# A masked sum moved into a later batch, a maximum over partitions by TensorE, and two activations in the other order

## What is computed

```python
x = x + tanh(g_xattn[0]) * attention0(layernorm(x), ctx)
x = x + tanh(g_ffn[0]) * ffn0(layernorm(x))      # base + update * 0.5
x = x + tanh(g_xattn[1]) * attention1(layernorm(x), ctx)
x = x + tanh(g_ffn[1]) * ffn1(layernorm(x))
# ffn0: the update goes through the sum over e of coefs[e] * mask[e] (e = 0, 1, 2)
# ffn1: x_scale = 448 / max(abs(x2)); w_scale = 448 / max(abs(weight))
#       out = fp8(x2 * x_scale) @ fp8(weight * w_scale) / (x_scale * w_scale)
```

## Time and profile before

| | us |
|---|---|
| median of 3 runs (lowest, highest) | 1494.67 (1492.06, 1496.3) |
| time of the profiled execution | 1496.8 |
| its span in the profile | 1495.1 |
| PE busy in the span | 1377.2 (92%) |
| DVE busy | 971.4 (65%) |
| ACT busy | 745.9 (50%) |
| POOL busy | 426.3 (29%) |

### The profile page before, as it was taken

One profiled execution on the slowest core, in us unless ns is written; L12 is line 12 of the kernel. 1 busy time (PEld: TensorE's weight loads), 2 busy tenths in 40 slices (PEclk: granted clock), 3 DMA queues, 4 the chain that ended last, 5 costly groups with the idle time before them and its releaser, 6 DMA issues. The chain is left out here.

```text
span 1495.1 us, 28528 instructions
## 1 busy us (share of the span) xinstructions
PE 1377.2 (92%) x10782; PEld 1120.8 (75%) x10782; DVE 971.4 (65%) x1564; ACT 745.9 (50%) x1881; POOL 426.3 (29%) x473
## 2 busy tenths in 40 slices
PE   6998789989989999987999999999779999999388
PEld 6998778979889898865888888888556666666144
DVE  4363277777767767565232256578567999998597
ACT  4231167766757767763111110113157777777396
POOL 0010001101010110010110232232358888887324
PEclk9999889999999999999999999999889999999789
DMA  6742454553544536464445452112332222221023
GB/s 224 244 155 85 90 126 117 139 146 77 145 110 120 147 96 167 125 197 150 166 167 197 157 210 99 56 36 84 113 81 65 62 64 64 63 64 43 1 85 141
DMA packets 127910, 174.93 MB, mean 117 GB/s; under 512 B 27799, under 2 KB 96919, under 8 KB 127792
## 3 DMA queue, kind: packets, MB, share of 16 engines
q1 hardware_dynamic: 127792, 173.26, 39.9%
HBM read 86.94 MB, written 35.29 MB: 82 GB/s over the span
## 5 line engine op out<-in xcount | busy, mean ns | idle before, releaser
L1148 ACT ACTIVATE a_prob<-a_psS,a_negmax 128x256 f32<-128x256 f32 x512 | 236.7, 483 | 158.6 <-DVE a_negmax L1063 158.4
L1063 DVE TENSOR_REDUCE a_negmax<-a_psS 128x4 f32<-128x1024 f32 x128 | 154.1, 1204 | 68.1 <-PE a_psS L956 66.5
L881 POOL COPY a_recip<-a_recip_head 128x256 f32<-128x256 f32 x64 | 25.6, 400 | 526.5 <-DVE a_recip_head L1113 526.5
L931 PE MATMUL a_psQ<-a_xT_hi,wide 128*128 128x256 f32 x912 | 170.9, 288 | 0.4
L1375 PE MATMUL m_psY<-wide,m_a_hi 128*128 128x512 f32 x512 | 159.3, 393 | 6.8 <-DVE m_a_lo L1423 6.8
L1375 PE MATMUL m_psY<-w_ffn,m_a_hi 128*128 128x512 f32 x512 | 158.3, 390 | 0.0
L966 PE MATMUL a_psT<-ident,a_prob 128*128 128x128 f32 x1024 | 138.0, 279 | 14.1 <-issue 6.1
L931 PEld LDWEIGHTS a_psQ<-a_xT_hi,wide 128*128 128x128 f32 x912 | 138.7, 189 | 9.1 <-issue 5.9
L1165 ACT COPY a_probT<-a_psT 128x512 f32<-128x512 f32 x208 | 115.8, 609 | 36.7 <-PE a_psT L966 35.6
L966 PEld LDWEIGHTS a_psT<-ident,a_prob 128*128 128x128 f32 x1024 | 116.7, 143 | 23.0 <-issue 12.7
L931 PE MATMUL a_psQ<-a_xT_lo,wide 128*128 128x256 f32 x456 | 127.5, 280 | 0.0
(11 more groups left out here) (233 smaller groups left out, 3013.9 us busy)
## 6 DMA issues: line engine op xcount, KB each, us to landing
a_q_stack<-a_q_hi SPq DMA_DIRECT2D x128, 128.0 KB, 2.6
a_q_stack<-a_q_lo SPq DMA_DIRECT2D x128, 128.0 KB, 2.6
c_raw<-lay_ctxT SPq DMA_DIRECT2D x16, 512.0 KB, 4.8
rows<-in_x SPq DMA_DIRECT2D x8, 1024.0 KB, 6.4
scratch_o<-a_oT SPq DMA_DIRECT2D x16, 512.0 KB, 3.0
m_x<-in_x SPq DMA_DIRECT2D x8, 1024.0 KB, 5.9
scratch_x<-m_x SPq DMA_DIRECT2D x8, 1024.0 KB, 5.1
b_q_stack<-b_q_hi SPq DMA_DIRECT2D x64, 128.0 KB, 2.3
```

What stands on the lines that cost most here:

```text
L881: nc.gpsimd.tensor_copy(recip[:, t % 2], recip_head[:, t % 2].unsqueeze(3).broadcast_to([P, TT, JH0, HD0])).then_inc(recip_ready, 1)
L931: last = nc.tensor.matmul(bank[:, 0:S], w[:, kt, t * P:(t + 1) * P], a[:, kt, :], start=(kt == 0 and w is wq.hi and a is xT_hi), stop=(kt ...
L1063: nc.vector.tensor_reduce(negmax[:, n % 2, :], psS[:, bank:bank + 2, :].rearrange("p a (j k) -> p (a j) k", k=S), AX_X, ALU.max, negate=Tr ...
L1148: last = nc.scalar.activation(prob[:, n % 2, j, :], psS[:, 2 * (n % 2) + j // 2, (j % 2) * S:(j % 2 + 1) * S], ACT.Exp, bias=negmax[:, n % ...
```

## The change

Three edits. The masked sum (its wait and its three operations on DVE) moves from before the loop of attention 0 into unit 6 of batch 6, behind that unit's normalising. In the last stage the maximum over partitions no longer goes to GpSimd: DVE spreads `part_max` along 128 columns (`max_wide`), PE transposes that tile into a bank of `psY`, and DVE reduces each row of it, which gives every partition the maximum; PE also waits for that reduction before its first products may use the bank. And ACT makes `shifted` ahead of `scaled`, each with a semaphore of its own, so that DVE's exponent form can start on the first.

```diff
@@ attn0_stage, vector
             maximum(0, 1)
-            dve.wait_ge(coefs_loaded, 16 * 4 * NE)
-            nc.vector.tensor_tensor(coefs[:, :, :, :], coefs[:, :, :, :], masks[:, :, :, :], ALU.mult).then_inc(masked_done, 1)
...
+            def masked_sum():
+                dve.wait_ge(coefs_loaded, 16 * 4 * NE)
...
+                        if n == 6 and final and u == 0:
+                            masked_sum()
@@ ffn1_stage, gpsimd
-            pool.wait_ge(quant.part_done, 2)
-            nc.gpsimd.partition_all_reduce(quant.all_max[:, 0:1], quant.part_max[:, 0:1], P, ABSMAX
-                                           ).then_inc(quant.all_done, 1)
@@ ffn1_stage, tensor
+            pe.wait_ge(max_spread, 1)
+            nc.tensor.transpose(psY[:, 0, 0, 0:P], max_wide[:, :], sh.ident[:, :]).then_inc(max_turned, 1)
             pe.wait_ge(ident_ready, 1)
             pe.wait_ge(quant.weight_loaded, 16)
+            pe.wait_ge(quant.all_done, 2)
@@ ffn1_stage, vector
+            dve.wait_ge(quant.part_done, 2)
+            nc.vector.tensor_copy(max_wide[:, :], quant.part_max[:, 0:1].broadcast_to([P, P])).then_inc(max_spread, 1)
+            dve.wait_ge(max_turned, 1)
+            nc.vector.tensor_reduce(quant.all_max[:, 0:1], psY[:, 0, 0, 0:P], AX_X, ALU.max).then_inc(quant.all_done, 1)
             quant.scale_of(nc, dve, 0, 2).then_inc(quant.steps, 1)
...
             def add_exponent(k):
                 dve.wait_ge(magic_ready, k + 1)
+                dve.wait_ge(scaled_ready, k + 1)
@@ ffn1_stage, scalar
-                for m, dst in enumerate((scaled, shifted)):
-                    last = nc.scalar.activation(dst[:, k % AHEAD, :], rows_of(k), ACT.Identity, bias=offset[:, m, b, t:t + 1],
-                                                scale=factor[:, m, b, t:t + 1])
-                last.then_inc(shifted_ready, 1)
+                for m, dst, ready in ((1, shifted, shifted_ready), (0, scaled, scaled_ready)):
+                    nc.scalar.activation(dst[:, k % AHEAD, :], rows_of(k), ACT.Identity, bias=offset[:, m, b, t:t + 1],
+                                         scale=factor[:, m, b, t:t + 1]).then_inc(ready, 1)
```

More of the change, by code:

```diff
@@ L1084, in _ @@
             maximum(0, 1)
-            dve.wait_ge(coefs_loaded, 16 * 4 * NE)
-            nc.vector.tensor_tensor(coefs[:, :, :, :], coefs[:, :, :, :], masks[:, :, :, :], ALU.mult).then_inc(masked_done, 1)
[L1087 to L1090, removed]
+            def masked_sum():
+                dve.wait_ge(coefs_loaded, 16 * 4 * NE)
+                nc.vector.tensor_tensor(coefs[:, :, :, :], coefs[:, :, :, :], masks[:, :, :, :], ALU.mult).then_inc(masked_done, 1)
+                dve.wait_ge(masked_done, 1)
+                nc.vector.tensor_tensor(wsum[:, :, :], coefs[:, 0, :, :], coefs[:, 1, :, :], ALU.add).then_inc(masked_done, 1)
+                dve.wait_ge(masked_done, 2)
+                nc.vector.tensor_tensor(wsum[:, :, :], wsum[:, :, :], coefs[:, 2, :, :], ALU.add).then_inc(summed, 1)
             def copy_update(quarter):
@@ L2190, in ffn1_stage @@
         ident16 = sb("ident16", [P, P], BF16)
+        max_wide = sb("max_wide", [P, P])
         factor = sb("factor", [P, 2, B, TT])
@@ L2204, in ffn1_stage @@
         ident_ready = sem("ident_ready")
+        max_spread, max_turned = sem("max_spread"), sem("max_turned")
+        scaled_ready = sem("scaled_ready")
         factors_ready, out_scale_ready = sem("factors_ready"), sem("out_scale_ready")
```

## The result

| | before | changed |
|---|---|---|
| median us (lowest to highest, runs) | 1493.37 (1491.77 to 1496.3, 4) | 1481.85 (1481.44 to 1482.54, 4) |
| profiled execution, us | 1496.8 | 1481.44 |
| its span, us | 1495.1 | 1479.7 |

The ratio is 0.9921 with a 95% interval from 0.9903 to 0.9939, a gain of 11.5 us on the medians. A second set of runs of the changed kernel, beside later runs of the one before, gave 1483.23 us and 0.9928 (0.9911 to 0.9945).

What follows compares the result with a forecast made beforehand. PE was taken to bound the kernel, so edits elsewhere count only where PE stands still for them. 5.9 - 0.8 + 5.1 + 0.9 = 11.1 us, from the median 1494.67 to 1483.6 us; range 1480 to 1488.

Steps and rivals of the forecast that it cites:

- the four distances: Stretches touched by the edits: start 5.9 us gained, batch 6 0.8 lost, last stage 5.1 and 0.9 gained.
- Part 1: Start of attention 0: without the masked sum PE's transposes of unit 2 come 5.9 us earlier, bounds 5.0 and 6.4.
- The step on the clock: Start of attention 0: clock rises at about 187.2, as long after PE's restart as before; 1.3 us more, partly ACT-limited.
- the stall: Start of attention 0: PE idle 5.06 us before its transposes of x, waiting for DVE's split; on PE's path.
- The Trainium skill's rule that transposes don't count as busy in the same way: Rival, start of attention 0: clock rise doesn't come early, term 5.1 us, time 1484.4; chance 0.10.
- Part 2: Batch 6, unit 7: the moved sum's 2.13 us less 1.29 cover stalls PE 0.84 us; loss between 0 and 1.8.
- Part 3: Last stage: maximum by PE takes 1.24 us instead of GpSimd's 6.34; gain 5.1 us, bounds 2.2 and 5.6.
- The upper bound of 5.6: Last stage, maximum by PE: gain 5.6 us if operations are as cheap as the 0.17 us reduction of 16 numbers.
- The rival that PE pays for entering the stage: Last stage: entry, not GpSimd's operation, costs the 6 us; maximum's gain 2.2 us, time 1486.5; chance 0.08.
- Part 4: Last stage, `shifted` first: first copy 6.82 us after ACT's first activation instead of 7.69; gain 0.87, from 0 to 1.0.
- the slower case: Rival, last stage: clock stays down behind PE's early lone transpose; 15 tiles cost 58 us, time 1542; chance 0.02.
- Nothing was given back in attention 0: Rival: ACT or `q_stack` copies become late, attention 0 returns half the start's gain; gain 8.1 us, time 1486.6; chance 0.10.

Runs made afterwards that it cites:

- the doubled reduction: The kernel before with GpSimd's reduction over partitions made twice in a row in the last stage, the second waiting for the first; one time taken, 1491.9 us.

## Why the prediction was right

**The time.** 1483.6 was told from the median of the runs then known, 1494.67, a gain of 11.1 us; measured are 11.5 and, in the second set, 9.2. That the first comes within 0.4 us is in part luck, since two sets of one kernel differed by 1.8. What carries the prediction is the four distances, each of which came out within 0.2 us of what was told.

**Part 1.** Told 5.9 us to PE's transposes of unit 2, with ACT as what lets no more through. Measured 5.9 at those transposes, and 5.5 to 6.0 at the fourth reciprocal, by which profiles are compared. PE started those transposes at 188.89, 9.91 us behind the first maximum (178.98 to 188.89) against 15.81 before (180.39 to 196.20). The step on the clock was off: the rise was told 3.6 us behind PE's restart and came 4.3 behind it (182.22 to 186.5). It cost nothing because ACT was the limit, as told: its copy ran from 188.15, and PE took up unit 2 at 188.89. The other kernels bear that out: in the eight profiles without the stall the clock rose 4.3 to 5.3 us behind this restart, and unit 2's transposes still started 9.9 to 10.1 us behind the first maximum. The Trainium skill's rule that transposes don't count as busy in the same way ("TensorE: Matmul & The Clock Gate", section Part 4: PE-mode transpose) would have had the rise put off. It was, by 0.7 us, but that doesn't single out this rule: in the six profiles with the stall, where PE does the same work behind its restart each time, the rise came anywhere from 3.4 to 5.1 us behind it. So the time to the rise isn't a constant that a sum may rest on.

**Part 2.** Told 0.84 us of PE wait, measured 0.74 in the wait and 0.8 in the batch; the cover was 1.38 us and not 1.29. That the maximum of unit 9 and the copy behind the sum add nothing held. What the prediction left out is that the clock in batch 7 may fall or not, 1.5 us at a time; whether the edit has a part in it stays open.

**Part 3.** Told 1.24 us for the three operations with their hops, measured 1.33 less the 0.17 of `part_max`, that is 1.16: the spread 0.23, PE's transpose 0.48 and the reduction 0.29 us. Gain told 5.1, measured 5.2. (The upper bound of 5.6 doesn't come out of the numbers that it names: both DVE operations at 0.17 us make it 5.3, all three at 0.17 make it 5.7. Nothing hung on it.) The rival that PE pays for entering the stage is out: its transpose began 0.05 us behind the spread's end. What GpSimd's 6 us were was told wrongly: the prediction took them for its operation, and the doubled reduction put 0.51 us on an operation and 5.5 on the first use. The gain didn't hang on it, since the edit removed the only use in the stage.

**Part 4.** Told 0.87 us, the first copy at T+6.82; measured 0.87 and T+6.81; PE's transposes came at T+5.58, told T+5.68. DVE's added waits did no harm; near the end its rounding still ended 1.2 us ahead of PE's transposes:

```profile
1467.55 1.22 DVE L119 SCALAR_TENSOR_TENSOR q_xq<-q_magic,q_total 128x1024 bf16<-128x1024 f32 x1
...
1469.99 0.61 PE L2255 MATMUL q_psT<-q_ident,q_xq 128*128 128x128 bf16 x8
```

**The other rivals.** The clock did rise in the last stage, so the slower case didn't come. Nothing was given back in attention 0 up to its last batch, with ACT nearly full.

## What to carry to other kernels

Before a time is predicted from one profile, get a second one of the same kernel: here the stages that no edit touched differed by one to two us each, more than two of the four terms of the sum. A small step moved to another place on its engine was free where that engine waited for something else, and the row with the idle time in front of it says how much fits (2.18 us took 2.12 whole, 1.38 us left 0.74 over). Where a reduction over partitions of one column stands on the path alone, a spread, a transpose and a reduction can replace it: here that took 1.16 us in place of 6.34. And a start that comes earlier isn't yet an end that comes earlier: of 0.66 us at the first copy nothing was left at the last output of the one profile taken, because the clock rose later.

## What the runs showed of the hardware

- GpSimd's reduction over partitions shows 0.41 us in its row. Its first use in the last stage comes 5.6 to 5.9 us behind the number that it waits for (six profiles), its use in the middle stage 5.5 to 5.8 us behind GpSimd's operation before it (14 profiles), and no row fills that time. A second one right behind the first starts 0.10 us after it.
- At the start of attention 0 the clock rose 3.4 to 5.1 us behind PE's restart in the six profiles with the stall, with the same work behind it, and 4.3 to 5.3 us in the eight without. Around one 2.6 us gap in batch 7 it fell in ten of 14 profiles, each time for 3.4 us and at a price of 1.5 us, and not in the other four.
- Short distances inside a stage repeat to 0.1 us from kernel to kernel (batch 6, the maximum's first use to the first copy, each with and without its edit). The long ones, with loop edges or the border of a stage in them, and those in which the clock rises, differ by up to 2 us.
